# A two-layer transformer block in fp32: attention outputs normalised on GpSimd, output projection without the multiply, value blocks redistributed over steps

## The chip, the cores and the metric

The kernel runs on one core of a Trainium2 chip. The core has TensorE (PE; its weight loads are listed apart as PEld), VectorE (DVE), ScalarE (ACT), GpSimd (POOL) and SyncE (SP), which here only issues DMAs. The metric is the device time of one execution in microseconds, the median of several runs.

## The reference, cut to what matters

Two layers over 2048 tokens of width 512, all in fp32. The part that the change touches is the softmax attention of the second layer (32 query heads, 8 key/value heads of width 64, two sequences of 1024 tokens as the kernel lays the tokens out, causal), its output projection, and the second matmul of the first layer's feed-forward:

```python
# first layer, feed-forward (16 blocks of 128 hidden units, masked by a top-4 router)
h = jax.nn.gelu(einsum('nf,ibf->nib', x, W1b), approximate=False) * mask[:, :, None]
y = einsum('nib,fib->nf', h, W2b)
# second layer, attention
scores = einsum('bhqd,bhkd->bhqk', q, kf) / sqrt(64)
attn = softmax(where(causal, scores, finfo.min), axis=-1)
out = einsum('bhqk,bhkd->bhqd', attn, v)
x = x + out.transpose(0, 2, 1, 3).reshape(b, s, 2048) @ o_w.T + ffn(x)
```

## The kernel before

The program is six stages, each a block of its own in which the five engines run their own instruction lists, joined by semaphores. At the end of a block all engines meet. The stages are the first attention, the first feed-forward (`feed_forward0`), the projections, the second attention (`attention1`), the output projection (`output1`) and the second feed-forward. Matmuls of full precision are made of three products of rounded parts (`split_matmul`, L47 to L52): high by high, high by low, low by high.

**feed_forward0** runs 16 iterations (4 groups q of hidden units by 4 chunks c of 512 tokens). In each, PE makes 4 hidden blocks (48 matmuls), ACT takes the gelu (L919), DVE multiplies by the mask into `h` (L1013), ACT rounds `h` to the high part (L923, counted by `h_hi`), POOL subtracts to get the low part (L940, counted by `h_lo`), and PE multiplies by W2 (48 matmuls, 12 for each block b). For block b PE waits for `h_lo` of b and then runs the three products of each of four token tiles. Beside this DVE unpacks the 4-bit weights of the second feed-forward (L969 to L988).

**attention1** handles 16 units u (8 key/value heads by 2 sequences), each of 24 steps, numbered through as n = 24u + r. Steps r = 0 to 15 are the long half (the last 512 queries of a sequence, one of the four heads in each step, up to 1024 keys), steps 16 to 23 the short half (the first 512 queries, two heads in each step). In step n PE makes the scores (`score(n)`: masks at L1752, products at L1755) into one of two PSUM pairs, so that `score(n)` waits until ACT has exponentiated step n-2. DVE takes the row maxima (L1692, L1695), ACT the exponentials with their row sums in `den` (L1662), and DVE, two steps later, transposes the 32x32 blocks of the result (L1710, L1713, L1715). At fixed steps counted from the start of the unit, PE also multiplies the transposed blocks by the values (`values`, L1770): a table names for each step which blocks of 32 keys it does, SHORT_VALUES for the short half and LONG_VALUES for the long one. Steps beyond 23 lie in the next unit, so that 26 is step 2 of the unit after. Short blocks 0 to 15 have 8, 8, ..., 8, 6, 4, 2 matmuls in the program (13, 14 and 15 the last three), over ever fewer queries; each matmul stands in the trace as two. ACT copies the sums out of PSUM in two pieces (`evict`, L1672; steps SHORT_LEFT and LONG_LEFT) into one of two buffers `o`, and SP stores them unnormalised to `OT`. At step INVERT (26) DVE takes the reciprocal of the row sums and transposes it (`invert`, L1721 and L1724), and SP stores it to `R`. SP runs down its own list in the order of n: query loads (L1577), keys (L1587), values (L1595), `store_o` (L1602), `store_r` (L1609).

**output1** is 32 steps n (2 sequences b by 16 pairs of heads k). SP loads a row tile of `OT` into `of` (L1870) and the matching inverses, spread over 64 partitions each, into `rd` (two DMAs, L1872), and for b = 0 a piece of the weights (L1865). DVE multiplies `of` by `rd` (L1921), ACT rounds the product to its high part (L1895), POOL subtracts for the low part (L1902), and PE runs 24 matmuls (8 token tiles by three products), after a wait on POOL's part. For b = 0 ACT and DVE also split the weights (L1890, L1916). What step 0 needs is loaded while attention1 ends. The rings of `of` and of the two parts are three deep.

## Time and profile before

| | |
|---|---|
| median of 3 runs | 2274.7 us (2269.36 to 2278.79) |
| the profiled execution, own time | 2273.54 us |
| its span, first to last instruction | 2271.8 us |
| mean granted TensorE clock | 0.964 |
| busy: PE, PEld, DVE, ACT, POOL | 92%, 65%, 69%, 37%, 16% |
| stage: first attention | 0 to about 320 us |
| first feed-forward | about 320 to 690 |
| projections | about 690 to 962 |
| second attention | 962 to 1762 |
| output projection | 1762 to 1958 |
| second feed-forward | 1958 to 2272 |

All times in the rows count from the start of the span. A busy PE is not a PE at its peak: matmuls are pipelined, and a matmul's listed duration contains its latency, so the distance from one start to the next tells its cost. A granted clock of 1.00 is TensorE at 2.4 GHz, one of 0.50 at 1.2 GHz. For each engine a wait names what ended it.

### The profile page before, as it was taken

Reading aid. Unit: us, or ns where it says so; the run is one execution under the profiler, and the core shown is the slowest. Engines: PE = TensorE matmul, PEld = TensorE weight load, DVE = VectorE, ACT = ScalarE, POOL = GpSimd, SP = SyncE. Lnnn points to the kernel's source line nnn. Section 1 sums busy time; section 2 is a strip of 40 time slices with the busy share of each in tenths; the row PEclk is TensorE's granted clock in tenths of the full one; section 3 lists DMA queues with packets and bytes.
Section 4 is the critical chain, followed back from the end, with each engine's and each line's share of the span. In section 5 each row is a group of like instructions: output and inputs, shape, how many; then the busy total and the mean of one; then the engine's idle time right before and its main releaser. Section 6 shows DMA issues by size and latency. Waiting matters only on the chain. (4 is left out here: it accounts for less than half of the span.)

```text
span 2271.8 us, 52890 instructions
## 1 busy us (share of the span) xinstructions
PE 2084.5 (92%) x21680; PEld 1472.5 (65%) x21680; DVE 1578.6 (69%) x2439; ACT 845.8 (37%) x1773; POOL 366.6 (16%) x249
## 2 busy tenths in 40 slices
PE   7999969999998999978998898998988899999998
PEld 5777748887786788734444444444445687787776
DVE  5544323699976345499989999999994462577776
ACT  4322122222223200055555655556553221234443
POOL 0111111323220155400000000000000344221111
PEclk9999989999998999979999999999998899999999
DMA  5122145344427633423333433333332999420101
GB/s 182 57 94 76 38 172 181 102 132 132 125 76 285 184 111 125 150 67 103 100 91 96 116 101 97 104 94 104 110 92 78 286 249 273 141 84 19 56 1 38
DMA packets 205019, 268.18 MB, mean 118 GB/s; under 512 B 42304, under 2 KB 123520, under 8 KB 202112
## 3 DMA queue, kind: packets, MB, share of 16 engines
q1 hardware_dynamic: 203936, 264.85, 38.4%
q8 instruction: 162, 2.65, 0.5%
q14 instruction: 57, 0.47, 0.1%
q10 hardware_dynamic: 864, 0.21, 0.0%
HBM read 181.81 MB, written 83.17 MB: 117 GB/s over the span
## 5 line engine op out<-in xcount | busy, mean ns | idle before, releaser
L1662 ACT ACTIVATE a_prob<-ps,a_nmax 128x256 f32<-128x256 f32 (+7 forms) x512 | 376.7, 738 | 326.9 <-DVE a_nmax L1692 228.7
L1755 PE MATMUL ps<-xacc 64*128 64x512 f32 (+5 forms) x1536 | 389.7, 550 | 80.8 <-ACT a_prob L1662 74.9
L1692 DVE TENSOR_REDUCE a_nmax<-ps 128x1 f32<-128x1024 f32 (+3 forms) x256 | 256.2, 1001 | 45.8 <-PE ps L1755 44.7
L1755 PEld LDWEIGHTS ps<-xacc 64*128 64x128 f32 x1536 | 146.4, 197 | 200.1 <-ACT a_prob L1662 118.4
L1713 DVE STREAM_TRANSPOSE a_pt_long<-a_prob 128x768 f32<-128x768 f32 (+1 forms) x256 | 238.0, 930 | 0.0
L2083 DVE SCALAR_TENSOR_TENSOR f_part<-ps,f_gu_scale,f_part 128x512 f32<-128x512 f32 x264 | 185.2, 746 | 66.9 <-PE ps L2130 53.5
L1770 PE MATMUL ps<-a_pt_long,xacc 32*64 32x256 f32 (+2 forms) x6144 | 211.7, 386 | 1.3 <-ACT a_o L1672 1.3
L1770 PEld LDWEIGHTS ps<-a_pt_long,xacc 32*64 32x64 f32 x6144 | 122.4, 137 | 109.5 <-issue 97.9
L940 POOL TENSOR_TENSOR f_hT_lo<-f_h,f_hT_hi 128x512 fp32r<-128x512 f32 x64 | 93.8, 1474 | 286.4 <-ACT f_hT_hi L923 286.4
L1902 POOL TENSOR_TENSOR o_oT_lo<-xacc,o_oT_hi 128x512 fp32r<-128x512 f32 x2 | 2.9, 1497 | 803.7 <-ACT o_oT_hi L1895 803.7
L1752 PE MATMUL ps<-xacc 64*128 64x128 bf16 x1024 | 113.8, 227 | 5.2 <-ACT a_prob L1662 5.0
L50 PE MATMUL ps<-o_wo_hi,o_oT_hi 128*128 128x512 f32 x256 | 103.2, 403 | 16.6 <-POOL o_oT_lo L1902 16.2
L1695 DVE TENSOR_REDUCE a_nmax<-ps 128x2 f32<-128x1024 f32 (+3 forms) x128 | 105.4, 823 | 17.0 <-PE ps L1755 15.0
L50 PE MATMUL ps<-f_xt_hi,f_w_hi 128*128 x256 | 100.6, 393 | 17.7 <-DMA f_xt_lo<-scratch_xt 17.7
L1710 DVE STREAM_TRANSPOSE a_pt_short<-a_prob 128x512 f32<-128x512 f32 (+3 forms) x256 | 114.1, 484 | 0.0
L1770 PEld LDWEIGHTS ps<-a_pt_short,xacc 32*64 32x64 f32 x3712 | 71.8, 134 | 60.6 <-issue 45.3
L1368 DVE TENSOR_TENSOR k_rp<-ps,k_cosq 128x512 f32<-128x512 f32 x64 | 43.9, 686 | 94.0 <-POOL k_qo L1245 78.7
L919 ACT ACTIVATE f_gl<-ps 128x512 f32<-128x512 f32 x64 | 38.1, 595 | 183.5 <-PE ps L52 183.5
L1245 POOL TENSOR_TENSOR k_qo<-k_rp 128x512 f32<-128x512 f32 x64 | 87.4, 1386 | 102.6 <-DVE k_rp L1368 102.6
L50 PE MATMUL ps<-f_w_hi,f_hT_hi 128*128 128x512 f32 x256 | 101.1, 395 | 2.9 <-POOL f_hT_lo L940 2.4
L51 PE MATMUL ps<-o_wo_lo,o_oT_hi 128*128 128x512 f32 x256 | 101.4, 396 | 0.0
L52 PE MATMUL ps<-o_wo_hi,o_oT_lo 128*128 128x512 f32 x256 | 101.2, 395 | 0.0
(234 smaller groups left out, 4489.7 us busy)
## 6 DMA issues: line engine op xcount, KB each, us to landing
xacc<-scratch_QT SPq DMA_DIRECT2D x512, 64.0 KB, 2.0
scratch_QT<-k_qo SPq DMA_DIRECT2D x64, 256.0 KB, 2.3
xacc<-scratch_V SPq DMA_DIRECT2D x64, 256.0 KB, 4.7
scratch_OT<-a_o SPq DMA_DIRECT2D x32, 512.0 KB, 5.0
o_of<-scratch_OT SPq DMA_DIRECT2D x31, 512.0 KB, 5.2
o_rd<-scratch_R SPq DMA_DIRECT2D x62, 256.0 KB, 8.0
f_block<-in_packed SPq DMA_DIRECT2D x33, 256.0 KB, 3.6
f_mask<-scratch_maskT SPq DMA_DIRECT2D x16, 512.0 KB, 5.1
```

The costliest lines, as they stand in the source:

```text
L50: pe.matmul(out, lh[lsel], rh[rsel], start=first, stop=False)
L51: pe.matmul(out, lh[lsel], rl[rsel], start=False, stop=False)
L52: return pe.matmul(out, ll[lsel], rh[rsel], start=False, stop=last)
L1662: last = nc.scalar.activation(prob[:, n % PRING, s].rearrange("p (a w) -> p a w", w=w), SC[n % 2][:, a, 0:w], ACT.Exp, bias=nmax[:, n % 4, ...
L1692: nc.vector.tensor_reduce(nmax[:, n % 4, 0:1], SC[n % 2][:, :, 0:width(0, t)], AX.XY, ALU.max, negate=True).then_inc(maxed, 1)
L1695: nc.vector.tensor_reduce(nmax[:, n % 4, :], SC[n % 2][:, :, 0:width(1, t)], AX.X, ALU.max, negate=True).then_inc(maxed, 1)
L1710: last = nc.vector.transpose(pt_short[:, 0:blocks, h, t, :], src)
L1713: last = nc.vector.transpose(pt_long[:, unit % 2, 0:near, h, t - 4, :], src[:, 0:near, :])
L1752: pe.matmul(sc[:, a, w - P:w], identb[r, s, :], causal[r, s, :], start=s == 0, stop=False, skip_group_check=True)
L1755: last = pe.matmul(sc[:, a, 0:w], q[r, slot, heads[a * hf], :], kt[r, b, keys], start=not masked, stop=True, skip_group_check=True)
L1770: last = pe.matmul(out[:, :, a - t0:4, :], v[rows, b, j, :], part[rows, c::2, a - p0:t0 + 4 - p0, :], start=j == 0, stop=j == BLOCKS[hf] - ...
L2083: nc.vector.scalar_tensor_tensor(part[:, s % 2, i, :], PB[(2 * k + i) % 4], gu_scale[:, s % NBK, i, k:k + 1], part[:, s % 2, i, :], ALU.mu ...
```

## The change

Five things are changed. **In attention1** POOL, idle there before, multiplies each evicted `o` in place by a spread table of inverses `rd` (128 x 1024, 31 times; the 32nd product is DVE's, at the end of the block), and SP stores `o` after that. `rd` is filled by two DMAs for each half (L1626 of the new kernel), issued by SP at steps 29 and 36, after `R` was stored. **The reciprocal** moves from step 26 to 25. **The short value blocks** go over six steps (26 to 31) in place of five, block 0 first and then from 15 down to 1; both pieces of the short half are evicted at step 32, and the stores come one step later. **In output1** the multiply and the loads of `rd` are gone, ACT rounds `of` straight from the load, and rows 0 and 1 are loaded during attention1. **In feed_forward0** PE waits for `h_hi` of block b, runs the eight matmuls that need the high part alone, then waits for `h_lo` and runs the other four.

```diff
@@ feed_forward0, tensor
-                            pe.wait_ge(h_lo.sem, h_lo.now(it, b + 1))
+                            pe.wait_ge(h_hi.sem, h_hi.now(it, b + 1))
                             for t in range(TPC):
                                 if b == 0:
                                     pe.wait_ge(y_added.sem, y_added.before(it, t + 1))
-                                last = split_matmul(pe, YB[t], hT, [w[:, p] for w in w2], b == 0, b == BPQ - 1,
-                                                    np.s_[:, b, t * P:(t + 1) * P], np.s_[:, b, :])
+                                part = hT[0][:, b, t * P:(t + 1) * P]
+                                for s in range(2):
+                                    pe.matmul(YB[t], part, w2[s][:, p, b, :], start=b == 0 and s == 0, stop=False)
+                            pe.wait_ge(h_lo.sem, h_lo.now(it, b + 1))
+                            for t in range(TPC):
+                                last = pe.matmul(YB[t], hT[1][:, b, t * P:(t + 1) * P], w2[0][:, p, b, :],
+                                                 start=False, stop=b == BPQ - 1)
@@ tables of attention1
-SHORT_VALUES = {26: range(0, 3), 27: range(3, 6), 28: range(6, 9), 29: range(9, 13), 30: range(13, 16)}
+SHORT_VALUES = {26: (0, 15, 14, 13, 12), 27: (11, 10, 9, 8), 28: (7, 6), 29: (5, 4), 30: (3, 2), 31: (1,)}
-SHORT_LEFT = {31: (0,), 32: (1,)}
+SHORT_LEFT = {32: (0, 1)}
-SHORT_STORE, LONG_STORE = 34, 50
-INVERT = USTEPS + 2
+SHORT_STORE, LONG_STORE = 35, 51
+SHORT_INVERSE, LONG_INVERSE = 29, 36
+INVERT = USTEPS + 1
@@ attention1, sync
                 def store_o(u, hf):
...
-                    sp.wait_ge(evicted, 2 * i + 2)
+                    sp.wait_ge(scaled, i + 1)
...
+                def load_inverse(u, hf):
+                    g, b = divmod(u, NB1)
+                    tok = slice(FIRST[hf] * P, (FIRST[hf] + 4) * P)
+                    sp.wait_ge(r_stored, 64 * (u + 1))
+                    wait(sp, scaled, order(u, hf))
+                    for a in range(2):
+                        sp.dma_start(rd[a * HD1:(a + 1) * HD1, :, :],
+                                     d["R"][g, b, a::2, tok].partition_broadcast(HD1)).then_inc(rd_in, 16)
...
+                for k in range(2):
+                    sp.dma_start(rows[k], d["OT"][k, :, 0:SEQ]).then_inc(ahead, 16)
@@ attention1, gpsimd (new), and the same product once on vector at the end
+                for i in range(2 * NU - 1):
+                    pool.wait_ge(evicted, 2 * i + 2)
+                    pool.wait_ge(rd_in, 32 * (i + 1))
+                    nc.gpsimd.tensor_tensor(o[:, i % 2].rearrange("p s t i q -> p s (t i q)"),
+                                            o[:, i % 2].rearrange("p s t i q -> p s (t i q)"), rd[:], ALU.mult
+                                            ).then_inc(scaled, 1)
@@ output1, sync
-                for n in range(1, NSTEP):
+                for n in range(2, NSTEP):
...
-                    if n >= 2:
-                        sp.wait_ge(scaled, through(n - 2))
                     sp.dma_start(of[:, n % 3, :], d["OT"][k, :, b * SEQ:(b + 1) * SEQ]).then_inc(o_in[n % 3], 16)
-                    for a in range(2):
-                        sp.dma_start(rd[a * HD1:(a + 1) * HD1, n % 2, :],
-                                     d["R"][k // 2, b, 2 * (k % 2) + a, :].partition_broadcast(HD1)
-                                     ).then_inc(o_in[n % 3], 16)
@@ output1, scalar
-                        act.wait_ge(scaled, through(n, i))
+                        if n >= 2:
+                            act.wait_ge(o_in[n % 3], 16 * (n // 3 + (1 if n % 3 == 2 else 0)))
@@ output1, vector
-                    for i, s in enumerate(pieces(n)):
-                        if n:
-                            dve.wait_ge(o_in[n % 3], 48 * (n // 3 + (1 if n % 3 else 0)))
-                        nc.vector.tensor_tensor(row(n, s), row(n, s), inverse(n, s), ALU.mult).then_inc(scaled, 1)
```

What the tables do is seen at three places. First DVE around the start of a unit, before: `a_nmax` are the row maxima, `a_pt_short` and `a_pt_long` the transposed parts, `a_rden` the reciprocal.

```order
L1692 TENSOR_REDUCE a_nmax<-ps 128x1
L1710 STREAM_TRANSPOSE a_pt_short<-a_prob 128x4x32 x2
L1692 TENSOR_REDUCE a_nmax<-ps 128x1
L1710 STREAM_TRANSPOSE a_pt_short<-a_prob 128x4x32 x2
L1692 TENSOR_REDUCE a_nmax<-ps 128x1
L1713 STREAM_TRANSPOSE a_pt_long<-a_prob 128x24x32
L1715 STREAM_TRANSPOSE a_pt_wide<-a_prob 128x8x32
L1721 RECIPROCAL a_rden<-a_den 128x32
L1724 STREAM_TRANSPOSE a_rdenT<-a_rden 128x32
L1692 TENSOR_REDUCE a_nmax<-ps 128x1
```

And in the changed kernel, at the same place:

```order
L1719 TENSOR_REDUCE a_nmax<-ps 128x1
L1737 STREAM_TRANSPOSE a_pt_short<-a_prob 128x4x32 x2
L1719 TENSOR_REDUCE a_nmax<-ps 128x1
L1737 STREAM_TRANSPOSE a_pt_short<-a_prob 128x4x32 x2
L1748 RECIPROCAL a_rden<-a_den 128x32
L1751 STREAM_TRANSPOSE a_rdenT<-a_rden 128x32
L1719 TENSOR_REDUCE a_nmax<-ps 128x1
L1740 STREAM_TRANSPOSE a_pt_long<-a_prob 128x24x32
L1742 STREAM_TRANSPOSE a_pt_wide<-a_prob 128x8x32
L1719 TENSOR_REDUCE a_nmax<-ps 128x1
```

The reciprocal and its transpose have moved from behind the third maximum of the unit (step 2) to behind the second (step 1). The second place is ACT in the same unit, before (`a_prob` are the exponentials, `a_o` the evictions):

```order
L1662 ACTIVATE a_prob,a_den<-ps,a_nmax 128x256 x4
L1662 ACTIVATE a_prob,a_den<-ps,a_nmax 128x128 x4
L1662 ACTIVATE a_prob,a_den<-ps,a_nmax 128x1024 x4
L1662 ACTIVATE a_prob,a_den<-ps,a_nmax 128x896 x4
L1672 ACTIVATE a_o<-ps 128x2x8x32
L1662 ACTIVATE a_prob,a_den<-ps,a_nmax 128x768
L1672 ACTIVATE a_o<-ps 128x2x8x32
L1662 ACTIVATE a_prob,a_den<-ps,a_nmax 128x768 x3
```

And now:

```order
L1680 ACTIVATE a_prob,a_den<-ps,a_nmax 128x256 x4
L1680 ACTIVATE a_prob,a_den<-ps,a_nmax 128x128 x4
L1680 ACTIVATE a_prob,a_den<-ps,a_nmax 128x1024 x4
L1680 ACTIVATE a_prob,a_den<-ps,a_nmax 128x896 x4
L1680 ACTIVATE a_prob,a_den<-ps,a_nmax 128x768
L1690 ACTIVATE a_o<-ps 128x2x8x32 x2
L1680 ACTIVATE a_prob,a_den<-ps,a_nmax 128x768 x3
```

The two pieces of the short eviction stand together behind the first exponential of 768 columns (step 8), and none stands between steps 7 and 8. The third place is PE from the last short blocks to the first long ones, steps 6 to 10. Before, from the blocks of step 6 on (`xacc` rows are the scores, the 64x2x32 rows are blocks 13 to 15):

```order
L1770 MATMUL ps<-a_pt_short,xacc 64x2x32 x12
L1755 MATMUL ps<-xacc 128x448
L1752 MATMUL ps<-xacc 128x128 x2
L1755 MATMUL ps<-xacc 128x448
L1755 MATMUL ps<-xacc 128x384
L1752 MATMUL ps<-xacc 128x128 x2
L1755 MATMUL ps<-xacc 128x384 x2
L1752 MATMUL ps<-xacc 128x128 x2
L1755 MATMUL ps<-xacc 128x384 x2
L1752 MATMUL ps<-xacc 128x128 x2
L1755 MATMUL ps<-xacc 128x384
L1770 MATMUL ps<-a_pt_long,xacc 64x256 x16
```

And now, from the block of step 7 on:

```order
L1804 MATMUL ps<-a_pt_short,xacc 64x2x96
L1804 MATMUL ps<-a_pt_short,xacc 64x256 x3
L1804 MATMUL ps<-a_pt_short,xacc 64x2x96
L1804 MATMUL ps<-a_pt_short,xacc 64x256 x3
L1789 MATMUL ps<-xacc 128x384
L1786 MATMUL ps<-xacc 128x128 x2
L1789 MATMUL ps<-xacc 128x384 x2
L1786 MATMUL ps<-xacc 128x128 x2
L1789 MATMUL ps<-xacc 128x384 x2
L1786 MATMUL ps<-xacc 128x128 x2
L1789 MATMUL ps<-xacc 128x384
L1804 MATMUL ps<-a_pt_long,xacc 64x256 x16
```

Blocks 3 and 2 (16 matmuls) stand ahead of these rows, behind the scores of step 6, and block 1 (8 matmuls) stands behind the scores of step 7, where none stood: two steps of scores alone are left between the short and the long blocks (8 and 9), and not three (7, 8 and 9).

## Rows read from the trace of the kernel before

**Rows 1.** The page of the profile: granted clock in 40 slices of the span.

```profile
PEclk9999989999998999979999999999998899999999
```

**Rows 2.** Busy time by stretch, whole stages (the first row names the columns).

```profile
core 0: us, PE busy (x) PEld busy (x) DVE busy (x) ACT busy (x) POOL busy (x), PEclk, DMA share, GB/s
...
962.00:1762.00 800.00, 706.06 (x14080) 376.16 (x14080) 709.14 (x1056) 444.26 (x1089) 0.00 (x0) 0.94 0.35 97
1762.00:1958.00 196.00, 182.64 (x769) 145.92 (x770) 85.79 (x66) 42.87 (x49) 77.01 (x33) 0.97 0.90 247
```

**Rows 3.** The same view of two units, from reciprocal to reciprocal.

```profile
1305.40:1354.40 49.00, 44.60 (x882) 23.22 (x880) 44.46 (x67) 27.62 (x69) 0.00 (x0) 0.93 0.36 100
1354.40:1401.00 46.60, 41.89 (x882) 22.40 (x880) 44.21 (x68) 27.77 (x70) 0.00 (x0) 1.00 0.38 105
```

**Rows 4.** The reciprocals of the 16 units: min/median/max ns, first and last start.

```profile
L1721 DVE RECIPROCAL a_rden<-a_den x16: 309/310/314, 1018.1 to 1730.9; 128x32 f32<-128x32 f32 x16
```

**Rows 5.** Timeline of PE at step 8 of an odd unit (start, us, what).

```profile
1410.41 0.56 PE L1755 MATMUL ps<-xacc 64*128 64x384 f32 x1 [1.18 <-ACT a_prob L1662]
```

**Rows 6.** Busy time by stretch: these steps, and what follows them.

```profile
1409.50:1413.00 3.50, 1.62 (x12) 0.79 (x12) 3.50 (x6) 2.35 (x5) 0.00 (x0) 0.99 0.52 137
1413.00:1419.80 6.80, 6.26 (x55) 2.40 (x60) 4.99 (x9) 3.46 (x7) 0.00 (x0) 0.50 0.07 19
```

**Rows 7.** Timeline of DVE in step 2 of a unit.

```profile
1352.06 1.23 DVE L1692 TENSOR_REDUCE a_nmax<-ps 128x1 f32<-128x1024 f32 x1 [0.66 <-PE ps L1755]
...
1354.41 0.31 DVE L1721 RECIPROCAL a_rden<-a_den 128x32 f32<-128x32 f32 x1
1354.76 0.21 DVE L1724 STREAM_TRANSPOSE a_rdenT<-a_rden 128x32 f32<-128x32 f32 x1
```

**Rows 8.** Timeline of ACT in steps 8 and 9 of a unit.

```profile
1367.52 0.59 ACT L1672 ACTIVATE a_o<-ps 128x512 f32<-128x512 f32 x1
1368.55 0.90 ACT L1662 ACTIVATE a_prob<-ps,a_nmax 128x768 f32<-128x768 f32 x1 [0.44 <-DVE a_nmax L1692]
```

**Rows 9.** Waits in the output projection (us in total, times, longest).

```profile
PE ps L50 <- POOL o_oT_lo L1902: 16.2, 9, 8.8
```

**Rows 10.** Groups by line in the output projection.

```profile
L1902 POOL TENSOR_TENSOR o_oT_lo<-o_of,o_oT_hi 128x1024 fp32r<-128x1024 f32 x31 | 74.1, 2389 | 108.1 <-ACT o_oT_hi L1895 108.1
...
L1921 DVE TENSOR_TENSOR o_of<-o_of,o_rd 128x1024 f32<-128x1024 f32 x31 | 41.1, 1325 | 74.8 <-DMA o_rd<-scratch_R 74.8
```

**Rows 11.** Busy time by stretch in the output projection: its start, and without waits.

```profile
1766.50:1771.60 5.10, 5.01 (x12) 3.99 (x13) 1.72 (x2) 0.93 (x1) 1.63 (x1) 0.52 0.92 257
...
1820.00:1868.00 48.00, 48.00 (x213) 39.77 (x212) 31.02 (x23) 12.66 (x15) 20.87 (x9) 1.00 0.99 256
```

**Rows 12.** Timeline of all engines from the first projection instruction to the first matmul.

```profile
1762.49 0.63 ACT L1890 ACTIVATE o_wo_hi<-xacc 128x512 fp32r<-128x512 f32 x1 [3.62 <-PEq L1565]
...
1763.76 1.28 DVE L1921 TENSOR_TENSOR xacc<-xacc 128x512 f32<-128x512 f32 x2
...
1765.18 2.95 POOL L1902 TENSOR_TENSOR o_oT_lo<-xacc,o_oT_hi 128x512 fp32r<-128x512 f32 x2 [803.71 <-ACT o_oT_hi L1895]
...
1766.59 0.76 PE L50 MATMUL ps<-o_wo_hi,o_oT_hi 128*128 128x512 f32 x1 [8.85 <-POOL o_oT_lo L1902]
```

**Rows 13.** Waits in six iterations of the first feed-forward.

```profile
PEld ps L50 <- POOL f_hT_lo L940: 7.8, 12, 0.9
DVE f_w_lo L951 <- ACT f_w_hi L905: 6.8, 5, 1.4
```

**Rows 14.** Busy time by stretch, one of these iterations.

```profile
510.90:533.83 22.93, 22.36 (x97) 17.88 (x96) 20.87 (x32) 5.75 (x10) 6.21 (x5) 1.00 0.44 131
```

**Rows 15.** By line, min/median/max ns, first and last start: DVE beside and without POOL.

```profile
L980 DVE SCALAR_TENSOR_TENSOR f_block<-f_mag,f_block x33: 691/693/1789, 422.3 to 657.2; 128x512 f32<-128x512 f32 x33
...
L1916 DVE TENSOR_TENSOR o_wo_lo<-o_stage,o_wo_hi x14: 1434/2466/2474, 1772.3 to 1849.5; 128x512 fp32r<-128x512 f32 x14
...
L1713 DVE STREAM_TRANSPOSE a_pt_long<-a_prob x256: 823/958/969, 969.5 to 1719.0; 128x768 f32<-128x768 f32 x96, 128x640 f32<-128x640 f32 x32
```

More of the change, by code:

```diff
@@ L1797, in output1_rooms @@
     stage = xacc[:, 0:2, :]
-    of, rd = [xacc[:, r:r + 2, :].rearrange("p r n -> p (r n)") for r in (3, 5)]
-    return stage, of, rd
+    rows = [xacc[:, r:r + 2, :].rearrange("p r n -> p (r n)") for r in (3, 5)]
+    return stage, rows
 def output1(nc, ps, d, xacc, early):
```

57 lines of the change are left out of this document (32 added, 25 removed).

## The prediction, made before the changed kernel was run

> **What bounds the kernel now.** I looked first at the busy time by stage [rows 2]. In the second attention (800 us) PE and DVE are both near their limit, 706.06 and 709.14 us, POOL does nothing and DMA is at 0.35. In the output projection (196 us) PE is busy for 182.64 us, but DMA is at 0.90. So the first stage is shared between two engines, and what helps it must take work from whichever is last at that step; the second is PE's if its inputs come in time.
>
> Then the granted clock [rows 1]: it dips again and again in the slices of the attention. The same view of single units shows the form of it [rows 3]: a unit takes 49.0 us at a mean clock of 0.93, the next 46.6 us at 1.00, with the same number of matmuls. One reciprocal stands in each unit, and the 16 reach from 1018.1 to 1730.9 us [rows 4]: 712.8 us. Fourteen pitches of 46.5 us and a last one of 43.2 (its short steps are followed by no further unit) would be 694.2. So 18.6 us are lost in 14 pitches, and with one more fall of the clock inside the last unit, at the 2.5 us of a pair of [rows 3], some 21 us go to a slower clock. Where it falls is in the timeline [rows 5]: after the last short block (step 6) PE has only scores to do in steps 7, 8 and 9, and sits idle ahead of those of steps 8, 9 and 10, 1.18 us the first time, waiting for ACT, which waits for DVE. Over 3.5 us of this PE was busy for 1.62 us, and in the 6.8 us that follow the clock is at 0.50, where the scores and first long blocks of step 10 cost double [rows 6]. In the even units the same idle time lies there and the clock does not fall: it is near whatever makes it fall, and chance of position decides.
>
> **The parts of the change.**
>
> *Short blocks over six steps, attention.* Scores alone now stand in steps 8 and 9 only. Step 7 gets block 1 (8 matmuls), which fills a good part of the 1.18 us in front of the scores of step 8 [rows 5]. Two idle gaps of about a microsecond remain where there were three. The bounds: no fall at all any more (gain 21 us) and as many as before (0). The stretch that can catch a fall is shorter by a third to a half, and since it was a near thing in half of the units, I take one fall in five or six units, three in all at 2.5 us: 21 - 7.5 = **13.5 us gained**. The other steps: the first short step has 28 matmuls with 8 wide ones where it had 24 wide ones, none has more PE work than DVE work beside it, so their order costs nothing; DVE is the cover (steps 2 to 9 have no DVE gap), and were it gone, 0.5 us more at step 6 would cost 8 us.
>
> *The reciprocal one step earlier.* At step 2 DVE does a maximum, two transposes and then the reciprocal pair, 1354.41 to 1354.90, with nothing between: 0.49 us on the path. Ahead of that step it sat idle for 0.66 us waiting for PE's scores [rows 7]. The pair now falls into this gap and fits, with 0.17 us to spare. Nobody waits longer for it: ACT needs the sums' buffer a unit later, and SP's store of R comes earlier. 0.49 x 15 units = **7.3 us gained**; none of it, if the scores of step 2 slip by more. PE does not eat it: its chain from step 10 on starts when step 8 is exponentiated, and that comes earlier by the same 0.49 us.
>
> *Both short evictions at step 8.* ACT evicts one piece at 1367.52 and is free 0.44 us before the next maximum comes [rows 8]. The second piece of 0.54 us goes behind the first, so ACT is late by 0.1 us, and the first long blocks (which wait for both) by 0 to 0.3 us; from there PE is busy without a gap to the end of the unit, so this stays. I take 0.1 x 15 = **1.5 us lost** (0 to 4.5).
>
> *The product on POOL.* 31 instructions of 128 x 1024 with two SBUF inputs; the nearest row is POOL's subtraction of the same form, 2.389 us [rows 10]. One comes after each eviction, 20 us or more before the buffer is needed again: hidden. What is queued behind it on POOL is nothing. What it does to DVE is the question. DVE instructions with two SBUF inputs stretch beside POOL: 0.69 to 1.79 us for one line, 2.47 us for another [rows 15]. In the attention DVE has maxima out of PSUM and transposes with one SBUF input. No row shows a transpose beside POOL. Bounds: 0, and 2 us for each product. A transpose of 768 columns takes 0.96 us [rows 15], that is one element in 1.25 ns, no sign of a doubled rate that would need a second port; I take 0. The Trainium skill, page "SBUF — State Buffer", section "Who interferes with whom", says that a DVE instruction with at most one SBUF input, outside the two-port modes, does not contend with GpSimd; no row here shows it for a transpose.
>
> *The loads of the table.* Two DMAs of 256 KB for each half, 1 MB in 46 us or 23 GB/s on top of 97 [rows 2], and four issues in a unit. The queue is SP's own, in order. Behind the first pair stand the keys of the next unit, needed 18 steps later; behind the second the queries of the last short row, not needed for two steps. The new wait for R stands three steps after its store. I take 0; the bound is the issue time, about 0.5 us for each, 2 us in a unit and 32 us in all, if each one delayed a query.
>
> *The end of the block.* The last eviction is followed by DVE's product before the store: 1.28 us for the same amount [rows 12], all on the path. Behind the block, the first projection matmul came 4.1 us after ACT's start (1762.49 to 1766.59), with a DVE product of two halves in the chain [rows 12]. Without it ACT rounds the first half at 1763.1 and POOL starts at about 1763.8 in place of 1765.18: 1.4 us. **Sum 0.**
>
> *The output projection.* A step is 24 matmuls; without waits 213 of them take 48.0 us, 0.226 us each [rows 11], so 768 take 173.6 us. From the first at 1766.6 the stage lasts 191.4 us: 17.8 us too many. The start at half clock costs 5.1 - 12 x 0.226 = 2.4 us [rows 11] and stays; about 2 us are the end of the block and stay. The rest is waiting for POOL [rows 9], which waits for ACT, which waits for DVE's product, which waits for the spread inverses, 74.8 us in all [rows 10]: they are half of the traffic of a step (512 of 1024 KB, besides 256 KB of weights). Now the traffic is 768 KB in a step and then 512, in 5.4 us, about 145 and 97 GB/s against the 247 it moved [rows 2]. The next late thing would be POOL, at 2.4 us [rows 10] of a step of 5.4. So **13 us gained** (8 to 15). DVE's split of the weights still stretches to 2.47 us beside POOL [rows 15]; it is needed once in a step, two steps early.
>
> *The first feed-forward.* PE waits for POOL's low part 12 times in six iterations [rows 13], and such an iteration takes 22.93 us against 96 x 0.226 = 21.7 us. But DVE is busy there for 20.87 us [rows 14], and waits besides up to 1.4 us in each for ACT's rounding of the next weights [rows 13]: with its short gaps it goes round in 22.9 us without PE. So earlier matmuls only move PE forward against DVE, once: by at most the time of POOL's subtraction, 1.3 to 1.5 us, and not six times 1.0 us. **1.4 us gained** (0 to 6).
>
> **The sum.** 13.5 + 7.3 - 1.5 + 0 + 13 + 1.4 = 33.7 us. The profiled execution took 2273.5 us, 1.2 us less than the median of the runs. 2273.5 - 33.7 = 2239.8; I give **2240**.
>
> **Rivals.**
>
> *The clock goes on falling* (0.19). The two gaps left are enough, and the pitch of the units locks to it again. Speaks for it: a unit of 49.0 us and one of 46.6 stand in turn [rows 3], so the position of the idle time repeats; against it, that the idle time gets shorter by a third. Then the 13.5 us are not there: 2253.
>
> *Another bound in the projection* (0.08), say the loads' latency or ACT's two roundings, gives back 10 of its 13 us: 2250.
>
> *SP is late with the queries* (0.06). If half of the bound of 32 us, and the waits for R beside it, are paid by PE at the short rows: 2240 + 24 = 2264, within the bound of no change.
>
> *POOL and DVE exclude each other in the attention too* (0.07). This is the one that ends on the other side. If a transpose waits for a running product, as the instructions of [rows 15] did, each product takes up to 2 us from a DVE that has only about 2 us of slack in a unit, all in the steps from 10 on, while the short product falls into steps 8 and 9, where DVE has none. 30 products x 2 us = 60 us: 2300. It decides from 1.1 us for each product on: below, the gains of 33.7 us carry it.
>
> *The forecast* (0.60), 2231 to 2249: with no fall of the clock 7.5 us less and the eviction free; with six or seven falls 9 us more.
>
> **The numbers.** The range should take in the forecast and the first two rivals: from 2229 (all falls gone, evictions free, 1 or 2 us more from the feed-forward) to 2258 (all falls there, the late eviction at 0.3 us). About half a per cent, 11 us, is what a measurement of this kernel can tell from no change. Faster by more: 0.60 + 0.19 + 0.08 and a little of the third, 0.88. The same: 0.05. Slower: 0.07.
>
> **What would show it.** In the trace of the changed kernel: units with a pitch of 46.1 us at clock 1.00, and no more than about three of 48.5; the idle time of DVE ahead of step 2's maximum down from 0.66 to under 0.2 us; transposes as long as before beside POOL's product (0.96 us); DMA at 0.5 to 0.6 in the projection and its 768 matmuls within 178 us; iterations of 22.9 us still in the first feed-forward, with its end about 1.4 us earlier. The forecast is wrong in its main term if the falls are where they were, and in its sign if a transpose of 768 columns takes 2 us or more.

## The result, and the profile after

The changed kernel takes 2243.47 us (median of 4, 2240.29 to 2248.74) against 2276.74 us for the kernel before, run beside it (median of 4, 2269.36 to 2279.35). The ratio is 0.9866, with a 95% interval of 0.9842 to 0.9890: faster by 1.3%. Forecast were 2240 us and a range of 2229 to 2258. The profiled execution took 2240.29 us, its span is 2238.5 us, 33.3 us less than that of before; the prediction's sum was 33.7.

The page's clock row of the kernel after (answers to [rows 1]):

```profile
PEclk9999989999998999989999999999999999999999
```

Busy time of its second attention and its output projection (answers to [rows 2]; columns: stretch, length, busy us and count of PE, PEld, DVE, ACT, POOL, granted clock, DMA share, GB/s):

```profile
960.10:1744.60 784.50, 692.95 (x14080) 365.92 (x14080) 709.53 (x1057) 443.54 (x1089) 73.00 (x31) 0.97 0.44 120
1744.60:1926.10 181.50, 175.99 (x769) 145.34 (x769) 44.05 (x33) 42.26 (x49) 77.98 (x33) 0.98 0.51 175
```

The attention, 800 us before, is 784.5; the projection, 196 before, is 181.5 with a DMA share of 0.51 in place of 0.90. To book the 33.3 us I compare the same PE events in both traces, the last matmul of each stage: 1.6 us come in the first attention, which the change doesn't touch, 0.5 in the first feed-forward and the projections, 15.2 in the second attention, 14.5 in the output projection, and 1.5 in the second feed-forward, untouched too. The untouched stages of the other kernels below scatter by as much (the first attention's last matmul stands at 288.1 to 290.1 us, the second feed-forward's matmuls take 294.3 to 296.2 us), so the 3.1 us of these two stages are within scatter, and no part of the forecast.

**The units.** Unit by unit, from one unit's first maximum to the next one's, a unit without a clock fall now takes 46.17 us; before it took 46.51. The same view of four units of the kernel after (answers to [rows 3]): the second row is an undisturbed one, the third has a fall of the clock in step 9, and the first and the last have a halt of PE and a fall in steps 3 and 4.

```profile
1103.00:1152.60 49.60, 44.45 (x884) 22.94 (x883) 44.53 (x67) 27.64 (x69) 4.71 (x2) 0.97 0.46 119
1340.20:1386.40 46.20, 42.08 (x883) 22.11 (x884) 44.16 (x66) 27.65 (x69) 4.70 (x2) 1.00 0.47 128
1432.60:1480.20 47.60, 43.56 (x884) 22.52 (x883) 44.49 (x67) 27.63 (x69) 4.71 (x2) 0.96 0.47 124
1620.40:1669.50 49.10, 43.89 (x882) 22.82 (x881) 44.36 (x66) 27.54 (x69) 4.71 (x2) 0.97 0.46 120
```

DVE in step 2 of a unit (answers to [rows 7]; start, length, what, idle time before it): the reciprocal and its transpose stand in step 1, and DVE idles for 0.18 us ahead of the next maximum, where it was 0.66.

```profile
1250.95 0.31 DVE L1748 RECIPROCAL a_rden<-a_den 128x32 f32<-128x32 f32 x1
1251.30 0.21 DVE L1751 STREAM_TRANSPOSE a_rdenT<-a_rden 128x32 f32<-128x32 f32 x1
1251.69 1.22 DVE L1719 TENSOR_REDUCE a_nmax<-ps 128x1 f32<-128x1024 f32 x1 [0.18 <-PE ps L1789]
```

**GpSimd's product.** The groups by line have its mean, 2355 ns (busy us, mean ns, idle time before it):

```profile
L1708 POOL TENSOR_TENSOR a_o<-a_o,a_rd 128x1024 f32<-128x1024 f32 x31 | 73.0, 2355 | 698.6 <-ACT a_o L1690 689.2 <-DMA a_rd<-scratch_R 9.4
```

The timeline of all engines in step 9 has one product from 1267.82 to 1270.19 us, and beside it transposes of 768 columns that take 0.96 us, as in [rows 15]:

```profile
1267.59 0.96 DVE L1740 STREAM_TRANSPOSE a_pt_long<-a_prob 128x768 f32<-128x768 f32 x1
...
1267.82 2.37 POOL L1708 TENSOR_TENSOR a_o<-a_o,a_rd 128x1024 f32<-128x1024 f32 x1 [16.70 <-ACT a_o L1690]
...
1269.50 0.96 DVE L1740 STREAM_TRANSPOSE a_pt_long<-a_prob 128x768 f32<-128x768 f32 x1
```

**The output projection.** Waits in it (answers to [rows 9], which had nine waits and 16.2 us; us in total, times, longest): only the first one, before the stage starts, is left.

```profile
PE ps L50 <- POOL o_oT_lo L1926: 8.6, 1, 8.6
```

**Halts of PE.** In steps 3 and 4 of four units (3, 4, 5 and 14) PE stands still for 0.93 to 1.78 us with nothing that the profile shows it to wait for ("issue"). The kernel before has two such halts, of 1.25 and 1.23 us, in units 4 and 5. In unit 3 the halt comes shortly after a run of 64 matmuls of the narrow blocks in 1.18 us (timeline of PE):

```profile
1108.92 1.18 PE L1804 MATMUL ps<-a_pt_short,xacc 32*64 32x64 f32 x64
...
1110.51 0.54 PE L1789 MATMUL ps<-xacc 64*128 64x448 f32 x1
1112.83 1.02 PE L1789 MATMUL ps<-xacc 64*128 64x448 f32 x2 [1.78 <-issue]
```

The view of three stretches of unit 14 shows what follows such a halt: the clock averages 0.59 over the next 4 us.

```profile
1620.40:1629.00 8.60, 5.58 (x135) 2.84 (x134) 8.31 (x14) 5.60 (x10) 2.35 (x1) 1.00 0.86 221
1629.00:1633.00 4.00, 3.94 (x45) 1.93 (x46) 1.74 (x2) 0.61 (x1) 0.00 (x0) 0.59 0.67 176
1633.00:1640.00 7.00, 6.50 (x103) 2.84 (x101) 6.57 (x10) 3.33 (x7) 0.00 (x0) 0.99 0.40 102
```

### The profile page after: what moved, and what is told of

Same layout as the page of the kernel before. It is cut to its first block and busy times, and to the rows that moved or that the text cites. A ratio compares the mean times of both kernels' runs of the same rounds, so it can differ in the third digit from the quotient of the medians.

```text
span 2238.5 us, 52908 instructions
## 1 busy us (share of the span) xinstructions
PE 2060.0 (92%) x21680; PEld 1458.7 (65%) x21680; DVE 1536.0 (69%) x2407; ACT 844.3 (38%) x1773; POOL 441.0 (20%) x280
## 5 line engine op out<-in xcount | busy, mean ns | idle before, releaser
L1789 PE MATMUL ps<-xacc 64*128 64x512 f32 (+5 forms) x1536 | 378.8, 535 | 74.0 <-ACT a_prob L1680 66.6
L1708 POOL TENSOR_TENSOR a_o<-a_o,a_rd 128x1024 f32<-128x1024 f32 x31 | 73.0, 2355 | 698.6 <-ACT a_o L1690 689.2
L1804 PE MATMUL ps<-a_pt_long,xacc 32*64 32x256 f32 (+2 forms) x6144 | 204.0, 374 | 2.1 <-ACT a_o L1690 1.3
L940 POOL TENSOR_TENSOR f_hT_lo<-f_h,f_hT_hi 128x512 fp32r<-128x512 f32 x64 | 94.1, 1480 | 284.2 <-ACT f_hT_hi L923 284.2
L1804 PEld LDWEIGHTS ps<-a_pt_short,xacc 32*64 32x64 f32 x3712 | 65.6, 135 | 75.6 <-issue 59.3
L2092 POOL TENSOR_TENSOR f_hT_lo<-f_h,f_hT_hi 128x512 fp32r<-128x512 f32 x44 | 57.6, 1308 | 254.8 <-ACT f_hT_hi L2048 254.8
L1804 PE MATMUL ps<-a_pt_short,xacc 32*64 32x192 f32 (+3 forms) x3712 | 100.1, 308 | 7.7 <-issue 5.3
```

The source lines that it names most:

```text
L1789: last = pe.matmul(sc[:, a, 0:w], q[r, slot, heads[a * hf], :], kt[r, b, keys], start=not masked, stop=True, skip_group_check=True)
L1804: last = pe.matmul(out[:, :, a - t0:4, :], v[rows, b, j, :], part[rows, c::2, a - p0:t0 + 4 - p0, :], start=j == 0, stop=j == (LONG_LAST, ...
```

## The experiments

The numbers of the second attention in each kernel's profile stand here together; e1 to e10 are the experiments below, each one the kernel after with the edit shown. "Clean" is the pitch of a unit without falls and halts; the sum covers the units 1 to 14; "loss" is that sum less 14 clean pitches; falls and halts (0.5 us or more) are counted in those units. In most kernels unit 1 is 1.1 to 1.7 us longer than a clean one (not in before, e5 and e7), which is in the loss.

| kernel | clean, us | units 1 to 14, us | loss | falls in steps 8, 9 | halts, steps 3, 4 | falls there |
|---|---|---|---|---|---|---|
| before | 46.51 | 669.5 | 18.4 | 7 | 2 | 0 |
| after | 46.17 | 660.5 | 14.1 | 3 | 4 | 2 |
| e1_old_table | 46.48 | 663.9 | 13.2 | 7 | 0 | 0 |
| e2_wide_first | 46.17 | 655.2 | 8.8 | 5 | 0 | 0 |
| e3_mixed_seven | 46.17 | 648.0 | 1.6 | 0 | 0 | 0 |
| e4_late_inverse | 46.65 | 667.5 | 14.4 | 5 | 5 | 1 |
| e5_long_early | 45.18 | 634.5 | 2.0 | 0 | 1 | 0 |
| e6_spare_loads | 46.17 | 662.0 | 15.6 | 5 | 3 | 2 |
| e7_old_ff_wait | 46.17 | 659.5 | 13.1 | 5 | 3 | 1 |
| e8_short_early | 46.02 | 648.7 | 4.4 | 1 | 0 | 0 |
| e9_small_product | 46.17 | 653.9 | 7.5 | 0 | 3 | 1 |
| e10_fill_eight | 46.17 | 653.2 | 6.8 | 0 | 3 | 1 |

### The old placement of the short blocks (e1)

```diff
-SHORT_VALUES = {26: (0, 15, 14, 13, 12), 27: (11, 10, 9, 8), 28: (7, 6), 29: (5, 4), 30: (3, 2), 31: (1,)}
+SHORT_VALUES = {26: (0, 1, 2), 27: (3, 4, 5), 28: (6, 7, 8), 29: (9, 10, 11, 12), 30: (13, 14, 15)}
```

> The changed kernel with the short value blocks placed as before (steps 26 to 30, block 0 to 15), all else as changed. Theory A (the idle gaps of PE in steps 7 to 9 make the clock fall, and block 1 in step 7 takes one of them away): the falls come back in about every second unit, 8 or more of 16, each costs 2 to 2.5 us, and the time is 2250 to 2258 us. Rival B (any change of a unit's length would have unlocked the falls, the placing of the blocks does nothing): at most 5 units with a fall, 2240 to 2246 us. The stalls of PE seen in step 3 of the changed kernel (1.8 and 1.6 us, with no engine to wait for) are gone from step 3 if they belong to the run of narrow blocks there.

Measured: 2249.13 us (2245.93 to 2250.79), ratio to before 0.9886 (0.9857 to 0.9915). Seven falls are back in steps 8 and 9, no unit halts, and the clean pitch is 46.48 us. The whole attention, first to last maximum, takes 758.0 us; before 764.5, after 752.0. So the new placement is worth 6.0 us, and nearly all of it has nothing to do with the clock: 0.31 us of each unit, 4.6 us in 15 pitches, come back without any fall. What the falls and halts cost in the units 1 to 14 is no more here (13.2 us) than in the kernel after (14.1). Theory A had the number of falls about right (seven, and an eighth in the last unit), but their price of 2 to 2.5 us holds for one only: six of the seven last 3.4 us, and the plain ones cost 1.4.

Where the 0.31 us lie is seen in step 2 (timeline, unit 6 of this kernel). The 24 wide matmuls of blocks 0 to 2, 48 in the trace, take 1.55 us, and DVE waits 0.18 us for the scores behind them. In the kernel after the blocks of that step take 1.18 us (56 matmuls in the trace), and DVE goes on without a gap.

```profile
1253.49 1.55 PE L1804 MATMUL ps<-a_pt_short,xacc 32*64 32x256 f32 x48
...
1256.21 1.22 DVE L1719 TENSOR_REDUCE a_nmax<-ps 128x1 f32<-128x1024 f32 x1 [0.18 <-PE ps L1789]
```

From the maximum of step 2 to that of step 3 it is 2.84 us in the kernel before, 2.62 here and 2.36 in the kernel after. With the blocks in their old order the earlier reciprocal alone would have brought less than half of its gain. I had priced the order of the blocks at nothing.

### Six steps, wide blocks first (e2)

```diff
-SHORT_VALUES = {26: (0, 15, 14, 13, 12), 27: (11, 10, 9, 8), 28: (7, 6), 29: (5, 4), 30: (3, 2), 31: (1,)}
+SHORT_VALUES = {26: (0, 1), 27: (2, 3), 28: (4, 5), 29: (6, 7), 30: (8, 9, 10), 31: (11, 12, 13, 14, 15)}
```

> The changed kernel with the short blocks over six steps in rising order: 0 and 1, 2 and 3, 4 and 5, 6 and 7, 8 to 10, 11 to 15. Step 7 is filled as well, now by the five narrowest blocks (34 matmuls), and the wide ones stand first. Theory A: few falls after step 8, as in the changed kernel. Theory C (PE's instruction stream runs dry where many short matmuls stand together): no stall in step 3, where only wide blocks stand now, and if any, one behind step 7. Together 2238 to 2244 us. If the stalls of step 3 stay, they have another cause, such as loads that run at that time.

Measured: 2238.73 us (2233.04 to 2239.99), ratio 0.9834 (0.9803 to 0.9864). The halts in steps 3 and 4 are gone and with them their falls, as theory C had it; five falls in step 9 stay, each 3.4 us long, and each lengthens its unit by 1.42 us (47.59 or 47.60 against 46.17). So there are two places for a fall, and one goes without the other.

### Seven steps, wide and narrow blocks mixed (e3)

```diff
-SHORT_VALUES = {26: (0, 15, 14, 13, 12), 27: (11, 10, 9, 8), 28: (7, 6), 29: (5, 4), 30: (3, 2), 31: (1,)}
+SHORT_VALUES = {26: (0, 13, 12), 27: (1, 11, 15), 28: (2, 10), 29: (3, 9), 30: (4, 8), 31: (5, 7), 32: (14, 6)}
```

> The changed kernel with the short blocks over seven steps, each step a wide and a narrow one (44 entries at most in a step, where the changed kernel has 56 and 64), so that scores alone stand in step 9 only. Theory A: no fall of the clock behind step 8 or 9. Theory C: no stall in step 3. Both together would take the units from a mean of 47.1 us to 46.2: 14 us less than the changed kernel, 2228 to 2234 us. Rival B: as many falls as in the changed kernel, 2240 to 2246 us.

Measured: 2232.10 us (2229.20 to 2233.70), ratio 0.9811 (0.9782 to 0.9839), as A and C together had it. Busy time over the units 1 to 14: a clock of 1.00 over the whole stretch.

```profile
1012.40:1660.40 648.00, 595.98 (x12323) 318.69 (x12321) 618.57 (x925) 386.34 (x951) 63.64 (x27) 1.00 0.47 127
```

Idle PE in front of the scores at the end of the short blocks, in the kernel after and then in this one (timeline, unit 6 of the one and unit 5 of the other): of two gaps of nearly a microsecond one is cut to 0.36 us by the blocks in step 8. The gap ahead of these two, 1.18 us in the kernel before, is 0.56 us in the kernel after and 0.34 here.

```profile
1265.02 0.59 PE L1789 MATMUL ps<-xacc 64*128 64x384 f32 x1 [0.97 <-ACT a_prob L1680]
...
1266.83 0.59 PE L1789 MATMUL ps<-xacc 64*128 64x384 f32 x1 [0.82 <-ACT a_prob L1680]
```

```profile
1215.65 0.59 PE L1789 MATMUL ps<-xacc 64*128 64x384 f32 x1 [0.36 <-ACT a_prob L1680]
...
1217.46 0.59 PE L1789 MATMUL ps<-xacc 64*128 64x384 f32 x1 [0.82 <-ACT a_prob L1680]
```

### The narrow run kept, step 8 filled (e10)

```diff
-SHORT_VALUES = {..., 30: (3, 2), 31: (1,)}
+SHORT_VALUES = {..., 30: (3,), 31: (2,), 32: (1,)}
```

> The placement of the kernel after in its first four steps (the dense run of narrow blocks 15 to 8 stays), but blocks 3, 2 and 1 in the steps 30, 31 and 32 one by one, so that step 8 holds a short block where it held scores alone. (A) Two separate causes: the falls in the steps 8 and 9 come from the idle gaps of 0.97 and 0.89 us there and vanish once step 8 is filled; the halts and falls in the steps 3 and 4 come from the narrow run and stay. Then no fall at step 9 in the units 2 to 13, one to three at step 3 or 4, attention 742 to 749 us, 2234 to 2241 us. (B) One cause, the narrow run: falls at step 9 come as in the kernel after, 750 us or more and 2241 to 2248 us. (C) The seven steps alone made the kernel with the mixed placement free of both: neither here, 739 to 741 us and 2230 to 2234 us.

Measured: 2239.65 us (2235.03 to 2242.13), ratio 0.9858 (0.9824 to 0.9892), attention 744.6 us. (A) in all its numbers. Busy time by stretch: the units 3 to 13 run at a mean clock of 1.00, unit 14 at 0.97.

```profile
1104.40:1614.50 510.10, 467.46 (x9684) 241.60 (x9685) 486.22 (x727) 304.25 (x749) 51.83 (x22) 1.00 0.47 128
1614.50:1663.70 49.20, 44.13 (x883) 22.69 (x883) 44.38 (x67) 27.64 (x69) 4.71 (x2) 0.97 0.46 120
```

The timeline of PE has the halt in that unit:

```profile
1623.21 0.43 PE L1804 MATMUL ps<-a_pt_short,xacc 32*64 32x128 f32 x3 [1.66 <-issue]
```

In six kernels with the narrow run (after, e4, e6, e7, e9, e10) unit 14 halts for 1.62 to 2.23 us in step 3 and the clock falls there, each time; in four with another order (e1, e2, e3, e8) no unit halts in steps 3 and 4. Two exceptions keep this from being the whole cause: the kernel before, with the old order, halts in two units by 1.25 and 1.23 us in step 4, though e1 with the same order never does, and e5 has one halt of 0.53 us. Neither is followed by a fall. And the order is not enough for a halt: in the units 1 to 14 all halts of all kernels stand in the units 3 to 6 and 14, though the same steps recur in every unit. The DMA share does not tell these units from others: over the first 8.6 us it is 0.86 to 0.89 in the units 3, 4 and 14 of the kernel after, 0.83 and 0.84 in its units 6, 9 and 11, which do not halt, and 0.87 in unit 14 of e3, which does not either.

### The reciprocal at its old step (e4)

```diff
-INVERT = USTEPS + 1
+INVERT = USTEPS + 2
```

> The changed kernel with the reciprocal at step 26 again. Theory (it lay on DVE's path at step 2 and lies in an idle gap of DVE at step 1 now): a unit without a fall takes 46.6 us and not 46.2, 7 us in all, 2248 to 2253 us, and the idle time of DVE ahead of step 2's maximum is 0.66 us again. Rival (PE sets the unit's length, and DVE's step does not count): 46.2 us and no difference.

Measured: 2253.44 us (2252.38 to 2254.95), ratio 0.9905 (0.9878 to 0.9932). The clean pitch rises from 46.17 to 46.65 us, 0.48 us, for a pair of instructions of 0.49, and DVE's idle time ahead of step 2's maximum is 0.65 us again. The step was right to a hundredth.

### Long blocks two steps earlier (e5)

Short blocks in five mixed steps, both evicted at step 30, and the long blocks spread from step 32 on:

```diff
-SHORT_VALUES = {26: (0, 15, 14, 13, 12), 27: (11, 10, 9, 8), 28: (7, 6), 29: (5, 4), 30: (3, 2), 31: (1,)}
+SHORT_VALUES = {26: (0, 11, 13, 15), 27: (1, 8, 14, 12), 28: (2, 7, 10), 29: (3, 6, 9), 30: (4, 5)}
-LONG_VALUES = {34: range(0, 2), 35: range(2, 4), 36: range(4, 6), 37: range(6, 8), 38: range(8, 10), ...}
+LONG_VALUES = {32: range(0, 2), 33: range(2, 4), 34: range(4, 5), 35: range(5, 7), 36: range(7, 8), 37: range(8, 10), ...}
-SHORT_LEFT = {32: (0, 1)}
+SHORT_LEFT = {30: (0, 1)}
```

> The kernel after with the sixteen short blocks in five steps (26 to 30) of mixed widths, {26: (0, 11, 13, 15), 27: (1, 8, 14, 12), 28: (2, 7, 10), 29: (3, 6, 9), 30: (4, 5)}, and the long blocks begun at step 32 and not 34. Beside the seven-step mixed placement (pitch 46.17 us, no clock fall in units 1 to 14, 2232.1 us), two theories. (A) The unit's length is set by TensorE in the steps 10 to 22, so that long-block work moved out of them into the steps 8 and 9 shortens every unit: pitch 45.2 to 45.7 us, attention 8 to 15 us shorter, 2217 to 2225 us. (B) The unit's length is the sum of TensorE's matmuls whatever step they stand in, or is set by another engine: pitch 46.0 to 46.3 us, and 2230 to 2236 us if no fall comes back; with falls of 3.4 us at five units, 2236 to 2245. I expect (B) slightly more than (A), since the kernel with seven steps had the same pitch as the one with five.

Measured: 2219.73 us (2216.00 to 2224.43), ratio 0.9757 (0.9725 to 0.9789). This beats both kernels. It is (A), at the strong end of its bounds and in the pitch just past it, where I had held (B) a little likelier: the pitch is 45.18 us, and the attention takes 725.0 us, 14.3 less than with seven steps and 27.0 less than in the kernel after. PE's waits for ACT over one undisturbed unit, in the kernel after and then here:

```profile
PE ps L1789 <- ACT a_prob L1680: 4.0, 5, 1.5
```

```profile
PE ps L1789 <- ACT a_prob L1680: 2.6, 3, 1.6
```

The steps 8 and 9 held waits for ACT and now hold blocks, and the steps 10 to 22, where PE is last, have that much less to do.

### The same short blocks, long blocks at their old steps (e8)

```diff
-LONG_VALUES = {32: range(0, 2), 33: range(2, 4), 34: range(4, 5), ...}
+LONG_VALUES = {34: range(0, 2), 35: range(2, 4), 36: range(4, 6), ...}
```

> The kernel before this one (long blocks from step 32, short blocks in five mixed steps: pitch 45.18 us, 2219.7 us) with the long blocks put back to step 34, so only the placement of the short blocks and their eviction at step 30 differ from the kernel after. (A) The gain of 1.0 us a unit came from taking long blocks out of the steps 10 to 22 into 8 and 9, which needs them begun at 32: here the pitch is 46.1 to 46.3 us, with no or few clock falls, attention 739 to 745 us, and 2230 to 2238 us. (B) It came from the five mixed steps themselves: pitch 45.1 to 45.5 us, 2219 to 2225 us.

Measured: 2234.90 us (2227.03 to 2241.32), ratio 0.9830 (0.9788 to 0.9873), clean pitch 46.02 us. (A) again, with a pitch 0.1 us below its bounds: of the 0.99 us that the kernel before this one (e5) gained in each unit, 0.84 belong to the long blocks and 0.15 to the short ones. These 0.15 us are the eviction. From the maximum of step 13 to that of step 14 it is 1.72 us here and in the kernel before, and 1.87 us in the six kernels compared that evict both pieces at step 8 (after, e1, e2, e3, e4, e10), whatever the order of their blocks: the first long blocks wait for both pieces and start 0.15 us later.

### The product cut to a hundredth (e9)

```diff
-                    nc.gpsimd.tensor_tensor(o[:, i % 2].rearrange("p s t i q -> p s (t i q)"),
-                                            o[:, i % 2].rearrange("p s t i q -> p s (t i q)"), rd[:], ALU.mult
+                    nc.gpsimd.tensor_tensor(o[:, i % 2].rearrange("p s t i q -> p s (t i q)")[:, :, 0:4],
+                                            o[:, i % 2].rearrange("p s t i q -> p s (t i q)")[:, :, 0:4], rd[:, :, 0:4], ALU.mult
```

> The kernel after, whose product on GpSimd in the second attention covers 4 of 512 columns of each half and not all of them (the normalisation is left out for the others), with all its waits and table loads in place. (A) The 31 products of 2.36 us cost nothing, as predicted: pitch 46.1 to 46.2 us without a fall, and 2238 to 2248 us, ratio 0.984 to 0.988. (B) They slow VectorE or delay the stores: the maxima of the steps 5 to 7 shorter, pitch at least 0.2 us less, 3 us or more off the whole, 2234 to 2240 us.

Measured: 2241.06 us (2236.03 to 2249.39), ratio 0.9861 (0.9820 to 0.9901). The other columns are left as they were evicted, so the result is not normalised. The clean pitch is 46.17 us with products of 0.20 us as with those of 2.36: they cost nothing. This is (A). DVE's transposes and maxima of the same form, here and then in the kernel after, are alike to 2 ns:

```profile
L1740 DVE STREAM_TRANSPOSE a_pt_long<-a_prob 128x768 f32<-128x768 f32 x186 | 178.4, 959 | 0.0
...
L1719 DVE TENSOR_REDUCE a_nmax<-ps 128x1 f32<-128x896 f32 x64 | 67.5, 1055 | 5.3 <-PE ps L1789 5.2
```

```profile
L1740 DVE STREAM_TRANSPOSE a_pt_long<-a_prob 128x768 f32<-128x768 f32 x183 | 175.7, 960 | 0.0
...
L1719 DVE TENSOR_REDUCE a_nmax<-ps 128x1 f32<-128x896 f32 x61 | 64.5, 1057 | 7.2 <-PE ps L1789 7.2
```

A side result: with the placement of the kernel after, this profile has no fall in steps 8 and 9, where three others with that placement (e4, e6, e7) have five and the kernel after three. The number of falls varies within one placement, and a count from a single profile proves little. Step 8 filled with blocks had none in 42 units (e3, e5, e10). But e8, which leaves the steps 7, 8 and 9 to scores alone as the kernel before does, with gaps of 0.72, 0.97 and 0.82 us, has a single fall in its 14.

### The loads of the table back in the projection (e6)

```diff
+                    if n >= 4:
+                        sp.wait_ge(o_high, through(n - 2))
+                    for a in range(2):
+                        sp.dma_start(rd[a * HD1:(a + 1) * HD1, n % 2, :],
+                                     d["R"][k // 2, b, 2 * (k % 2) + a, :].partition_broadcast(HD1)
+                                     ).then_inc(o_in[n % 3], 16)
...
-                            act.wait_ge(o_in[n % 3], 16 * (n // 3 + (1 if n % 3 == 2 else 0)))
+                            act.wait_ge(o_in[n % 3], 48 * (n // 3 + (1 if n % 3 == 2 else 0)))
```

> The kernel after, whose output projection loads the spread table R again as the kernel before did, and waits for it ahead of each split, but multiplies nothing: the DMA traffic and its wait are back, the multiplication and its place in the chain are not. (A) The stage was bound before by the chain of engines that the multiplication stood in (the prediction's step): the output projection stays at 177 to 179 us and the whole at 2243 to 2247 us, ratio to before 0.985 to 0.988. (B) The stage was bound by its transfers, and the gain came from their going: the stage is back near 188 to 191 us, the whole at 2254 to 2258 us, ratio 0.991 to 0.993.

Measured: 2252.37 us (median of 10, 2247.54 to 2269.28), ratio 0.9915 (0.9888 to 0.9942). From the start of the stage's first matmul to that of its last it is 181.8 us; 175.6 in the kernel after (175.5 to 176.7 in the others with its projection), 189.8 in the kernel before. Neither theory: of the 14.2 us, 6.2 come back with the traffic (5.1 against the slowest of the others), and 8.1 are what else the change took out, which is the multiplication and its place in the chain, with the second row tile now loaded ahead. Busy time by stretch, two for the first half of the stage and one for the second:

```profile
1756.20:1802.00 45.80, 43.69 (x185) 35.66 (x186) 9.13 (x8) 10.98 (x14) 18.67 (x8) 0.97 1.03 301
1802.00:1848.00 46.00, 43.82 (x187) 35.81 (x186) 18.53 (x10) 13.20 (x16) 21.49 (x9) 0.96 1.04 260
1848.00:1938.00 90.00, 90.00 (x399) 74.51 (x397) 8.41 (x13) 15.91 (x15) 35.95 (x15) 1.00 0.87 234
```

The loads cost something only in the first half, where weights are loaded besides: two waits of PE, 4.3 us together, and a fall of the clock. In the second half all 90 us are busy, with the loads of the table but without the product. The DMA share alone does not tell why: the third quarter, 1848 to 1893 us, has 1.03 too and no wait. The kernel before has three waits of 4.3 us together in its first half as well, and four more of 2.9 us in its second, which with the same loads are gone here.

### The old wait in the first feed-forward (e7)

```diff
-                            pe.wait_ge(h_hi.sem, h_hi.now(it, b + 1))
+                            pe.wait_ge(h_lo.sem, h_lo.now(it, b + 1))
                             for t in range(TPC):
...
+                                last = split_matmul(pe, YB[t], hT, [w[:, p] for w in w2], b == 0, b == BPQ - 1,
+                                                    np.s_[:, b, t * P:(t + 1) * P], np.s_[:, b, :])
```

> The kernel after, whose first feed-forward waits for h_lo ahead of all matmuls of a block again, as before. (A) The stage is bound by VectorE's queue there, so the moved wait gives little: its end 0.2 to 0.5 us later (that is what the kernel after gained in that window), the whole 2243 to 2245 us. (B) The split wait is worth 1.4 us as predicted and something else took it back in the kernel after: the stage 1.2 to 1.6 us longer than in the kernel after. Read from the stage's window in the profile, since the time alone can't tell so little.

Measured: 2245.68 us (2238.59 to 2254.62), ratio 0.9874 (0.9832 to 0.9916): too wide to tell. The profiles do. From the first matmul on `h` to the last, the stage takes 343.4 us here and in the kernel before, and 341.6 or 341.7 in every kernel with the split wait: 1.7 us, about what (B) had. But what comes next takes part of them back. PE's wait for the normalised rows ahead of the projections, in the kernel after, then with the old wait (us in total, times, longest):

```profile
PE ps L1393 <- DVE k_xn L1321: 9.7, 4, 9.1
```

```profile
PE ps L1388 <- DVE k_xn L1316: 8.6, 4, 7.9
```

DVE, whose queue those rows stand in, is not 1.7 us earlier, and 1.1 us go into this wait. Counted from the first matmul on `h`, the first one of the next stage comes after 351.7 us here, 351.8 in the kernel before and 351.1 in every kernel with the split wait: 0.6 us are left there. The first one on the query weights comes after 446.3 us here, 446.4 in the kernel before and 446.0 in the kernel after, but the others with the split wait spread from 445.6 to 446.5, so by then no gain can be told from none. (B) was right for the stage, (A) for the whole.

## Why the prediction was right, and where it was not

*Short blocks over six steps, 13.5 us forecast.* This is the step that failed: with the rest of the change in place (e1) the placement is worth 6.0 us of attention, and 4.6 of these are not the clock. Two parts of the working were wrong. "Their order costs nothing": I had compared the PE work of each step with the DVE work beside it as it was. Once the reciprocal is out of step 2, the 1.55 us of wide matmuls there make the next scores late, and the new order takes 0.31 us out of each unit. "Three in all at 2.5 us": three falls in steps 8 and 9 did come (the two without a halt beside them cost 1.4 us each), but two more came in steps 3 and 4 behind halts, in units 3.4 and 3.0 us longer than a clean one. So the rival "the clock goes on falling" was half right, at a place that it did not name. e2 and e10 take the two places apart, and e3 has neither.

Before and after compared, the attention gained 15.2 us. 5.1 of these (15 x 0.34) are the clean pitch and some 10 us the clock and the halts: 4.3 in the units 1 to 14 (loss 18.4 to 14.1), 2.8 in the tail behind the last maximum, the rest in the first and the last unit. That is near the 13.5 by luck. The kernel with the old placement (e1) has lost only 13.2 us in the same units, with seven falls as before. The difference is their length: five of the seven falls of the kernel before last 6.8 us and cost some 2.5 us each where no halt is beside them, and one of the seven of e1 does. Which part of the change made them shorter, or whether only their position in time did, is not shown. And the tail takes 24.6 to 31.3 us in these kernels, 28.6 in e7 with the same attention as the kernel after, so its 2.8 us are within scatter.

*The reciprocal, 7.3 us.* Right in its size (e4: 0.48 us a unit), in its place (idle time of 0.18 us left, forecast 0.17) and in its reason. It needs the new order of the blocks, though: in e1, with the early reciprocal and the old order, the step gained only 0.22 us and the next one lost 0.04.

*The late eviction, 1.5 us lost.* 46.51 less 0.48 would be 46.03; measured are 46.17. The step from 13 to 14 is longer by 0.15 us in every kernel compared that evicts both pieces at step 8, and not in e8, which evicts at step 6 and has 46.02. So it is 0.15 us a unit or 2.2 us in all, inside the bounds of 0 to 4.5, at the place forecast. The 46.48 us of e1 are this 0.15 and the 0.31 of the old order on top of 46.02.

*The product on POOL, 0.* Right: e9 has the same pitch with a hundredth of it. The Trainium skill, page "SBUF — State Buffer", section "Who interferes with whom", has it that a DVE instruction with at most one SBUF input, outside the two-port modes, doesn't contend with GpSimd. The prediction had no row for it; the trace after agrees, with 0.96 us for a transpose of 768 columns beside the product. The rival that ended on the other side (2300 us) is out.

*The loads of the table, 0.* No wait of PE for a DMA stands in the attention. Right.

*The output projection, 13 us.* 14.2 us between its first and last matmul. The limit of POOL was read rightly, and the rival of another bound is out. (The clean rate, 48.0 us for 213 matmuls, is 0.225 and not 0.226 us each, 0.5 us in the stage.) The cause was given as one chain, from the loads to the product; e6 shows two things that add, some 5 to 6 us of traffic in the first half and 8.1 us with the product.

*The first feed-forward, 1.4 us.* Gained: 1.7 us of its own matmuls, and 1.1 lost at the next wait. "Earlier matmuls only move PE forward against DVE, once" was the right reason; what failed is that this once would reach the end, since the next stage waits for the same DVE.

*The sum.* 33.7 forecast, 33.3 measured: closer than its parts, which is luck. (The upper end of the range, 2258, is some 2 us above what its terms give, 2239.8 + 13.5 + 3.) The attention fell short by 4.1 us (19.3 forecast, 15.2 measured), the feed-forward by 0.9; the projection with the wait ahead of it gave 1.5 us more (14.5), and 3.1 us came from stages that the change doesn't touch.

## What to carry to other kernels

Where two engines share a stage, look at each step for which of them is last: taking work from steps where PE is last and giving it to those where it waits brought 14.9 us here (e5 against e8), besides the 12.7 us that the falls and halts were worth (e3 against the kernel after). Idle gaps of PE can be paid twice, once as waiting and again when the clock falls behind them (1.42 us for a fall of 3.4 us), so fill them before counting them. Take out one edit at a time before naming what a gain came from: the term that was right in size before and after compared had another cause when its edit alone was undone. A pair of edits can also need each other, as the early reciprocal and the order of the blocks did. And when a stage is sped up that feeds another through the same engine's queue, follow the gain past the stage's end before booking it.

## What was not expected of the hardware

PE halted for 0.5 to 2.2 us without waiting for any engine, 24 times in the units 1 to 14 of the twelve kernels: 21 of these stand in the six kernels with a run of some 60 matmuls of the narrow blocks in about 1.2 us, two in the kernel before and one in e5, and all of them in the units 3 to 6 and 14. Spread among wide blocks, the same matmuls brought no halt in e3 and e8. Whether its instructions came late, or what else the place in the program has to do with it, was not shown.

A clock fall does not need a long idle time. It followed gaps of at most 1.18 us each in the kernel before, and of 0.97 and 0.82 us in the one after; with the first of the two cut to about 0.36 us it did not come in 28 units (e3, e10). The size of the gaps does not decide alone. A gap of 1.46 us (1.57 in e5) stands at the start of each clean unit, with no fall behind it, and the gaps that brought five falls in e2 (0.19, 0.97 and 0.82 us) are smaller than those that brought one in e8. The falls of e2 come in every third unit at first (4, 7, 10, 13), those of the kernel before in every second (7, 9, 11, 13), which points at a part of their position in time; no run tested it.
